# Two layers of a convolution network on one core: layer 1 moves into the bank of the input products, and steps move between ScalarE, VectorE and GpSimd

## The chip, the core and the metric

The kernel runs on one core of a Trainium2 chip. The metric is the device time of one execution in microseconds; the median of several executions counts. The core has a matrix engine (TensorE, PE in the rows), a vector engine (VectorE, DVE), a scalar engine (ScalarE, ACT) and GpSimd (POOL), each with its own queue that is worked off in order; SyncE (SP) starts transfers. The engines wait for each other by semaphores. Matrix products land in PSUM, eight banks of 512 float32 per partition.

## What is computed

The input x has 16 images of 128 channels and 128 x 128 pixels, float32. Cut to what matters:

```python
def _gn(v): ...            # mean and variance over groups of 4 channels and all pixels of an image

def layer0(x):             # x = _gn(x)
    xh = conv1x1(x, w_in, b_in)                       # 128 -> 256 channels
    pooled = jnp.mean(xh, axis=(2, 3))
    hcx = relu(pooled @ kg_w1.T + kg_b1)
    kernels = (hcx @ kg_w2.T + kg_b2)                 # a 3x3 kernel per image and channel
    y = depthwise_conv3x3(xh, kernels)
    y = y * jnp.tanh(softplus(y))                     # mish
    return conv1x1(y, w_out, b_out)                   # 256 -> 128

def layer1(x):             # x = _gn(x); FFT over channels, two 1x1 maps, inverse FFT
    return relu(real(ifft(...)))                      # linear up to the relu: one 128x128 matrix

x = x + layer0(_gn(x))
x = x + layer1(_gn(x))
```

## The kernel before

An image is a batch of 16 strips of 8 rows (1024 pixels); a half is 4 rows, 512 pixels. There are 256 strips n in all, and for each strip every engine runs one slot: `slot(n)` is written out for each engine by hand, and the order in it is the order of its queue. s = n % 16 is the strip's place in its batch. Layer 1 follows 19 strips behind: m = n - 19. Strips stay in SBUF (`X`, 23 places) from load to store.

The 256 hidden channels are split. The upper 128 get their nine taps as elementwise work on `xh`: the first three on ScalarE (`tap_product`, L407, into `tsum` and `tprod`), the two sums of these on GpSimd (`tap_add`, L1118), the other six on VectorE (`tap`, L907, in the two-bank `accB`). Of the lower 128 channels, the left SIDE = 56 of 128 columns are made the same way: ScalarE's `first_tap_side` (L416) and eight `side_tap` on VectorE (L919) in `accS`. The other 72 columns go through TensorE: `conv` (L654) multiplies the input, split in two float16 parts `hi` and `lo`, by tap matrices `wa` that hold kernel times input weight, three matmuls a tap, 27 a half.

The slot of TensorE for strip n, with the time-setting waits: `conv(n, 0)`; `layer1(m, 0)` (L705) into `psL`, waits for the ReLU before it; `product_out(n-1, 0)` (L696), the first layer's output product, into `psO`, waits for the Mishes of strip n-1 and the residual that read `psO` last; `product_b(n+2, 0)` (L674 to L676), the product of x, into `psB`; `conv(n, 1)` with `product_b(n+2, 1)` in its middle; `product_side(n+2)` (L685 to L687), also in `psB`; `layer1(m, 1)`; `product_out(n-1, 1)`. `psB` and `psO` are one bank each, and so is `psL`.

ScalarE's slot: `mish_side(n-1)` (L436), `first_tap_side(n)`, `mish_conv(n-1, 1)` (L429), `squares_1(n-2)` (L462), `tap_product(n+1, 0)` and `(n+1, 1)`, `mish_conv(n, 0)`, `relu(m, 0)` (L471), `sum_x` (L450), `evacuate(n+2, 0)` (L380, with an edge row L365 in some strips), `tap_product(n+1, 2)`, `squares_x` (L454), `evacuate(n+2, 1)`, `mish_taps(n)` (L442), `evacuate_side(n+2)` (L390), `relu(m, 1)`. VectorE's slot: `tap(n, 1)`, `residual(n-2, 1)` (L929), then side taps and taps in turn, `residual(n-1, 0)` between the sixth and the seventh side tap. GpSimd's slot: `add(m-1, 1)` (L1122), `cast(n+2)` (L1110), `tap_add(n+1, 1)`, `add(m, 0)`, `tap_add(n+1, 2)`, and the load of `hi` for strip n+3 (L1100).

In slots 10 to 15 of a batch, and slot 0 of the next, the weights for the next batch are made from its statistics: moments and group sums (10), the root on GpSimd (11), mean product and hidden layer (12: `pooled_products`, `hidden`), kernel products (13: `kernels`, L608), and three times `spread` (TensorE, L621), `tap_matrices` (VectorE, L876) and `taps_halves` (GpSimd: a float16 copy L1078 and the remainder L1080). In slots 1 to 3 the same goes on for layer 1's statistics. At the start, with nothing to overlap it, this chain is run once for batch 0, after `bn_stats` on 32 halves (L941). The last 16 strips of layer 1 are done behind the last slot.

## Time and profile before

| | us |
|---|---|
| median of 3 runs | 3799.29 |
| lowest, highest | 3797.97, 3801.11 |
| the profiled execution | 3798.16 |
| its span, first to last instruction | 3796.4 |

| engine | busy us | share of the span | instructions |
|---|---|---|---|
| TensorE | 3658.1 | 96% | 21868 |
| VectorE | 3522.8 | 93% | 4778 |
| ScalarE | 3316.2 | 87% | 5860 |
| GpSimd | 2774.9 | 73% | 2388 |

The busy time of an engine is the time in which at least one of its instructions was under way. Successive instructions overlap a little, so a row's duration is longer than what the instruction adds to its queue; the distance between two starts tells what it adds. Matmuls overlap most: their rows hold the way through the array. A row of a timeline ends in brackets with the idle time before it and who ended it, where there was some. Slots can be told apart by the second `product_out`, TensorE's last instruction of a slot.

### The profile page before, as it was taken

To read this page: it belongs to the slowest core of one execution; us is meant where nothing else is said; L and a number is where in the kernel's file an instruction comes from. 1 tells how busy PE (TensorE), PEld (TensorE's weight loads), DVE (VectorE), ACT (ScalarE), POOL (GpSimd) and SP (SyncE) were. 2 spreads that over 40 slices of the span, in tenths; PEclk is the share of its full clock that TensorE was granted. 3 is DMA by queue.
4 is the path that set the end of the run, shared out by engine and by line. 5 is a ranking of instruction groups with operands and counts; after the bars stand their busy time and mean duration, and the time that the engine had idled before them with its cause. 6 is when DMAs were issued, how large, how long until landed. Compare 5 with 4: busy or idle time off the path is not lost. (4 is left out here: it accounts for less than half of the span.)

```text
span 3796.4 us, 65618 instructions
## 1 busy us (share of the span) xinstructions
PE 3658.1 (96%) x21868; PEld 2251.8 (59%) x21868; DVE 3522.8 (93%) x4778; ACT 3316.2 (87%) x5860; POOL 2774.9 (73%) x2388
## 2 busy tenths in 40 slices
PE   4899999999999999999999999999999999999997
PEld 2455666656566666666656666565666656666664
DVE  5999999999999999999999999999999999999996
ACT  3888989899898998989999898998989989897775
POOL 3566777877778777777777777777777777777773
PEclk8999999999999999999999999999999999999999
DMA  4323444444444444444444444444444444443333
GB/s 152 78 70 104 130 128 132 125 130 131 122 139 119 137 127 127 136 122 132 126 128 132 128 130 125 131 133 123 134 128 129 130 125 134 125 131 95 92 94 126
DMA packets 148159, 468.99 MB, mean 124 GB/s; under 512 B 17328, under 2 KB 18416, under 8 KB 147568
## 3 DMA queue, kind: packets, MB, share of 16 engines
q1 hardware_dynamic: 110960, 397.66, 30.1%
q0 software_dynamic: 36864, 67.13, 12.2%
q8 instruction: 178, 2.92, 0.3%
q14 instruction: 157, 1.29, 0.1%
HBM read 397.61 MB, written 134.22 MB: 140 GB/s over the span
## 5 line engine op out<-in xcount | busy, mean ns | idle before, releaser
L654 PE MATMUL psA<-hi,wa 128*128 128x288 f16 (+4 forms) x9792 | 1852.2, 280 | 0.8 <-DVE wtmp L876 0.8
L907 DVE SCALAR_TENSOR_TENSOR accB<-xh,vectors,accB 128x1024 f32<-128x1024 f32 x1280 | 1640.4, 1282 | 0.0
L1118 POOL TENSOR_TENSOR tsum<-tsum,tprod 128x1024 f32<-128x1024 f32 x512 | 1210.5, 2364 | 293.9 <-ACT tprod L407 271.2
L919 DVE SCALAR_TENSOR_TENSOR accS<-side,vectors,accS 128x448 f32<-128x448 f32 x2048 | 1399.1, 683 | 19.2 <-ACT accS L416 10.0
L654 PE MATMUL psA<-lo,wa 128*128 128x288 f16 (+5 forms) x4896 | 1320.6, 279 | 0.0
L654 PEld LDWEIGHTS psA<-hi,wa 128*128 128x128 f16 x9792 | 931.0, 98 | 336.6 <-issue 66.9
L696 PE MATMUL psBO<-wm,woutt 128*128 128x512 f32 x2048 | 966.4, 594 | 12.5 <-DVE X L929 11.8
L1122 POOL TENSOR_TENSOR X<-X,zt 128x512 f32<-128x512 f32 x480 | 610.9, 1273 | 363.3 <-DVE accB L907 289.5
L696 PEld LDWEIGHTS psBO<-wm,woutt 128*128 128x128 f32 x2048 | 385.4, 190 | 497.5 <-issue 496.6
L1110 POOL TENSOR_TENSOR lo<-X,hi 128x1024 f16<-128x1024 f32 x256 | 546.9, 2136 | 182.6 <-DMA hi<-in_x_dram 111.4
L407 ACT ACTIVATE tprod<-xh,vectors 128x1024 f32<-128x1024 f32 x512 | 583.2, 1139 | 32.6 <-POOL tsum L1118 32.5
L654 PEld LDWEIGHTS psA<-lo,wa 128*128 128x128 f16 x4896 | 468.7, 98 | 238.2 <-issue 90.6
L705 PE MATMUL psL<-X,lpt 128*128 128x512 f32 x960 | 490.5, 592 | 2.3 <-ACT zt L471 2.3
L929 DVE SCALAR_TENSOR_TENSOR X<-psBO,vectors,X 128x512 f32<-128x512 f32 x512 | 382.5, 747 | 111.7 <-PE psBO L696 109.7
L380 ACT ACTIVATE xh<-psBO,vectors 128x512 f32<-128x512 f32 x510 | 348.7, 684 | 106.3 <-PE psBO L676 104.5
L907 DVE SCALAR_TENSOR_TENSOR accB<-xh,vectors,tsum 128x1024 f32<-128x1024 f32 x256 | 332.9, 1300 | 57.8 <-ACT wm L442 48.7
L471 ACT ACTIVATE zt<-psL,vectors 128x512 f32<-128x512 f32 x480 | 329.0, 685 | 42.1 <-PE psL L705 30.8
L407 ACT ACTIVATE tsum<-xh,vectors 128x1024 f32<-128x1024 f32 x256 | 290.7, 1136 | 3.9 <-DVE accB L907 3.4
L442 ACT ACTIVATE wm<-accB 128x1024 f32<-128x1024 f32 x256 | 261.8, 1023 | 27.9 <-DVE accB L907 27.0
L462 ACT ACTIVATE tprod<-X 128x1024 f32<-128x1024 f32 x256 | 270.5, 1057 | 13.3
L450 ACT ACTIVATE XS<-XS 128x1024 f32<-128x1024 f32 x240 | 252.8, 1053 | 3.8 <-DMA XS<-in_x_dram 3.7
L429 ACT ACTIVATE wm<-psA,vectors 128x284 f32<-128x284 f32 x480 | 231.1, 481 | 27.3 <-PE psA L654 26.6
(166 smaller groups left out, 3363.4 us busy)
## 6 DMA issues: line engine op xcount, KB each, us to landing
X<-in_x_dram SPq DMA_DIRECT2D x256, 512.0 KB, 3.3
out_dram<-X SPq DMA_DIRECT2D x256, 512.0 KB, 2.6
XS<-in_x_dram SPq DMA_DIRECT2D x240, 512.0 KB, 3.3
hi<-in_x_dram POOLq DMA_DIRECT2D x256, 256.0 KB, 4.3
X<-in_w_t_dram SPq DMA_DIRECT2D x2, 1152.0 KB, 18.3
w1t<-in_w_t_dram SPq DMA_DIRECT2D x1, 256.0 KB, 2.7
wint<-in_w_in_t_dram SPq DMA_DIRECT2D x1, 128.0 KB, 2.3
woutt<-in_w_out_t_dram SPq DMA_DIRECT2D x1, 128.0 KB, 2.6
```

The lines of the kernel that those rows point to most:

```text
L380: act(xh[:, r0:r0 + 4, 1:1 + W], ps, ACT.Identity, bias=b1).then_inc(s_xe, 1)
L407: act(rows_of(dst[:]), xh[:, 8 * j:8 * j + 8, k:k + W], ACT.Copy, scale=kk[i % 2][:, TAPS + k:TAPS + k + 1]).then_inc(done, 1)
L471: act(zt[:, t, :], psL[:], ACT.Relu, bias=lb[:, i % 2:i % 2 + 1]).then_inc(s_re, 1)
L654: last = mm(o[:, r:r + q, 0:cols], w, src[:, at:at + q, SIDE + dx - 1:SIDE + dx - 1 + cols], start=(tap == ORDER[0] and w is wh and src is ...
L696: last = mm(psO, woutt[:, h, :], wm[:, n % 2, h, t * TP:(t + 1) * TP], start=(h == 0), stop=(h == 1))
L705: mm(psL[:], lpt[:, i % 2, :], half(m, t), start=True, stop=True).then_inc(s_lm, 1)
L907: V.scalar_tensor_tensor(out=rows_of(accB[:]), in0=xh[:, 8 * j + dy:8 * j + dy + 8, dx:dx + W], scalar=kk[i % 2][:, TAPS + k:TAPS + k + 1] ...
L919: V.scalar_tensor_tensor(out=side_out(), in0=side[:, 8 * j + dy:8 * j + dy + 8, dx:dx + SIDE], scalar=kk[i % 2][:, k:k + 1], in1=side_out( ...
L929: V.scalar_tensor_tensor(out=half(n, t), in0=psO, scalar=boutp[:, 0:1], in1=half(n, t), op0=ALU.add, op1=ALU.add, accum_out=sum1[:, k:k + ...
L1110: P.tensor_tensor(lo[:, 8 * j:8 * j + 8, :], rows_of(strip(n)), hi[:, 8 * j:8 * j + 8, :], ALU.subtract).then_inc(s_lo, 1)
L1118: P.tensor_tensor(tsum[:], tsum[:], tprod[:], ALU.add).then_inc(s_ta, 1)
L1122: P.tensor_tensor(half(m, t), half(m, t), zt[:, t, :], ALU.add).then_inc(s_add, 1)
```

## The change

- SIDE goes from 56 to 60: 68 columns remain for TensorE, whose convolution matmuls have 272 columns instead of 288; side taps have 480 elements instead of 448, side products 488 columns instead of 456.
- `psO` becomes a tensor of two banks, and `residual` one operation on 1024 elements for two on 512. It runs in the place of the former half 1; `product_out` waits for it in half 0 alone.
- `psB` and `psL` become one bank, `psBL`. `product_b(n+2, 0)` waits for `relu(m, 0)`, and `layer1(m, 1)` for `evacuate_side(n+2)`. `product_out(n-1, 1)` goes ahead of `layer1(m, 1)`.
- The float16 copies of the tap matrices and input weights (`taps_halves`, `weights_halves`) move from GpSimd to ScalarE as `taps_high` and `weights_high`; GpSimd keeps the remainders, `taps_low` and `weights_low`.
- `tap_product(n+1, 1)` keeps its place before `mish_conv(n, 0)`, with `taps_high` before or behind it; `kernels_out` goes behind `mish_conv(n, 0)`; `small_0` behind the whole of `conv(n, 0)`.
- At the start the two loads of `w2t` go ahead of strips 2 to 15, and its copy and remainder ahead of the statistics' end. ScalarE's three `taps_high(0, u)` stand ahead of the first evacuations.
- Four `tensor_scalar` on GpSimd become `tensor_tensor` with a broadcast operand.

The diff, cut to its core:

```diff
-SIDE = 56
+SIDE = 60
@@
-        psBO = pb("psBO", [C, 2, TP])
-        psB, psO = psBO[:, 0, :], psBO[:, 1, :]
+        psO = pb("psO", [C, SP])
         accS = pb("accS", [C, TP])
-        psL = pb("psL", [C, TP])
+        psBL = pb("psBL", [C, TP])
+        psB, psL = psBL[:], psBL[:]
@@ sync
                 if n == 1:
                     for dst, src in consts:
                         eng.dma_start(dst, src).then_inc(s_const, 16)
-            for k in range(2):
-                eng.dma_start(w2t[:, k], w2_t[:, k]).then_inc(s_w2in[k], 16)
+                    for k in range(2):
+                        eng.dma_start(w2t[:, k], w2_t[:, k]).then_inc(s_w2in[k], 16)
@@ scalar
+            def taps_high(i, u):
+                eng.wait_ge(s_wt, 3 * i + u + 1)
+                act(wa[:, i % 2, 0, 3 * u * C:3 * (u + 1) * C], wtmp[:], ACT.Copy).then_inc(s_wsh, 1)
@@
-            stats_group("x", 0, small_bank(0))
-            pooled_out(0, small_bank(0))
-            hidden_out(0, small_bank(0))
             for k in range(2):
                 eng.wait_ge(s_w2in[k], 16)
                 act(w2p[:, 0, k], w2t[:, k], ACT.Copy).then_inc(s_w2h, 1)
+            stats_group("x", 0, small_bank(0))
+            pooled_out(0, small_bank(0))
+            weights_high(0)
+            hidden_out(0, small_bank(0))
             kernels_out(0, small_bank(0))
             bias_out(0, small_bank(0))
+            for u in range(3):
+                taps_high(0, u)
@@
                 if n + 1 < N:
                     tap_product(n + 1, 0)
+                if s == 0 and b >= 1:
+                    taps_high(b, 2)
+                if n + 1 < N:
+                    tap_product(n + 1, 1)
                 if s == 12 and build:
+                    weights_high(b + 1)
                     pooled_out(b + 1, small_bank(1))
                 if s == 3 and b >= 1:
                     layer1_bias(b - 1, small_bank(1))
-                if n + 1 < N:
-                    tap_product(n + 1, 1)
+                if s in (14, 15) and build:
+                    taps_high(b + 1, s - 14)
+                mish_conv(n, 0)
                 if s == 13 and build:
                     kernels_out(b + 1, small_bank(1))
-                mish_conv(n, 0)
@@ tensor, product_b
-                if bank is None:
+                if bank is None and t == 0 and n - 2 >= LAG1:
+                    eng.wait_ge(s_re, 2 * (n - 2 - LAG1) + 1)
+                elif bank is None:
                     eng.wait_ge(s_xe, 3 * n + t)
@@ product_out
-                if n + t >= 1:
-                    eng.wait_ge(s_x1, 2 * n + t)
+                if n >= 1 and t == 0:
+                    eng.wait_ge(s_x1, n)
@@ layer1
-                if m + t >= 1:
+                if t == 1 and m + LAG1 + 2 < N:
+                    eng.wait_ge(s_xe, 3 * (m + LAG1 + 2) + 3)
+                elif m + t >= 1:
                     eng.wait_ge(s_re, 2 * m + t)
@@ slot
-                conv(n, 0, slice(0, 5))
+                first = n % STRIPS == 0
+                conv(n, 0, slice(0, 6 if first else TAPS))
                 small_0(n)
-                first = n % STRIPS == 0
-                conv(n, 0, slice(5, 6 if first else TAPS))
@@
                     product_side(n + 2)
+                if n >= 1:
+                    product_out(n - 1, 1)
                 if m >= 0:
                     layer1(m, 1)
-                if n >= 1:
-                    product_out(n - 1, 1)
@@ vector
+                if c in (16, 20):
+                    k = (c - 16) // 4
+                    eng.wait_ge(s_w2h, k + 1)
+                    V.tensor_tensor(w2p[:, 1, k], w2t[:, k], w2p[:, 0, k], ALU.subtract).then_inc(s_w2l, 1)
@@
-            def residual(n, t):
-                eng.wait_ge(s_om, 2 * n + t + 1)
+            def residual(n):
+                eng.wait_ge(s_om, 2 * n + 2)
@@
-                    residual(n - 2, 1)
+                    residual(n - 2)
@@
-                if n >= 1:
-                    residual(n - 1, 0)
@@ gpsimd
-            def taps_halves(i, u):
-                k, part = 3 * i + u + 1, slice(3 * u * C, 3 * (u + 1) * C)
-                eng.wait_ge(s_wt, k)
-                P.tensor_copy(wa[:, i % 2, 0, part], wtmp[:]).then_inc(s_wsh, 1)
-                eng.wait_ge(s_wsh, k)
+            def taps_low(i, u):
+                part = slice(3 * u * C, 3 * (u + 1) * C)
+                eng.wait_ge(s_wsh, 3 * i + u + 1)
                 P.tensor_tensor(wa[:, i % 2, 1, part], wtmp[:], wa[:, i % 2, 0, part], ALU.subtract).then_inc(s_wsl, 1)
@@
                 eng.wait_ge(s_tap, NB * n + 1)
                 if s == 0 and b >= 1:
-                    taps_halves(b, 2)
+                    taps_low(b, 2)
```

TensorE's queue at the end of a slot, before. L685 to L687 are the side product, L705 is layer 1, L696 the output product, s_re counts ReLUs, s_xe evacuations and s_x1 residuals:

```order
L685 MATMUL psBO<-hi,wb 128x456 [waits s_xe]
L686 MATMUL psBO<-lo,wb 128x456
L687 MATMUL psBO<-hi,wb 128x456
L705 MATMUL psL<-X,lpt 128x512 [waits s_re]
L696 MATMUL psBO<-wm,woutt 128x512 [waits s_wS,s_x1,s_wB,s_wa]
L696 MATMUL psBO<-wm,woutt 128x512
L654 MATMUL psA<-hi,wa 128x288 [waits s_lo,s_wa]
```

The same place after the change:

```order
L704 MATMUL psBL<-hi,wb 128x488 [waits s_xe]
L705 MATMUL psBL<-lo,wb 128x488
L706 MATMUL psBL<-hi,wb 128x488
L715 MATMUL psO<-wm,woutt 128x512 [waits s_wS,s_wB,s_wa]
L715 MATMUL psO<-wm,woutt 128x512
L726 MATMUL psBL<-X,lpt 128x512 [waits s_xe]
L670 MATMUL psA<-hi,wa 128x272 [waits s_lo,s_wa]
```

Layer 1's second half has moved behind the output product and waits for the side's evacuation. In the middle of the slot, where half 0 of layer 1, half 0 of the output product and the first product of x follow each other, before:

```order
L705 MATMUL psL<-X,lpt 128x512 [waits s_re]
L696 MATMUL psBO<-wm,woutt 128x512 [waits s_wS,s_x1,s_wB,s_wa]
L696 MATMUL psBO<-wm,woutt 128x512
L674 MATMUL psBO<-hi,wb 128x512 [waits s_xe,s_lo]
L675 MATMUL psBO<-lo,wb 128x512
```

and after:

```order
L726 MATMUL psBL<-X,lpt 128x512 [waits s_re]
L715 MATMUL psO<-wm,woutt 128x512 [waits s_wS,s_x1,s_wB,s_wa]
L715 MATMUL psO<-wm,woutt 128x512
L693 MATMUL psBL<-hi,wb 128x512 [waits s_re,s_lo]
L694 MATMUL psBL<-lo,wb 128x512
```

The rows stand in the same order; the product of x waits for a ReLU in place of an evacuation. ScalarE's queue in slot 0 of a batch after the change; L415 are tap products, L354 is `taps_high`, L435 the convolution's Mish, L479 the ReLU of half 0:

```order
L444 ACTIVATE wm<-accS 128x8x60 [waits s_st,s_om]
L424 ACTIVATE accS<-side,vectors 128x480 [waits s_wS,s_kk,s_xe]
L435 ACTIVATE wm<-psA,vectors 128x4x68 [waits s_cv,s_om]
L470 ACTIVATE tprod,vectors<-X 128x1024 [waits s_ta,s_x1]
L415 ACTIVATE tsum<-xh,vectors 128x1024 [waits s_tap,s_kk,s_xe]
L354 ACTIVATE wa<-wtmp 128x384 [waits s_wt]
L415 ACTIVATE tprod<-xh,vectors 128x1024 [waits s_b1,s_kk,s_xe]
L435 ACTIVATE wm<-psA,vectors 128x4x68 [waits s_cv,s_om]
L479 ACTIVATE zt<-psBL,vectors 128x512 [waits s_add,s_lm]
```

The row of L354 is new there; before, the copy was GpSimd's first work of that slot.

## Rows read from the trace of the kernel before

**Rows 1.** The page, part 1: busy us, share of the span, instructions

```profile
PE 3658.1 (96%) x21868; PEld 2251.8 (59%) x21868; DVE 3522.8 (93%) x4778; ACT 3316.2 (87%) x5860; POOL 2774.9 (73%) x2388
```

**Rows 2.** Chain of waits, from 3600 to 3632: start us, us, what

```profile
3601.11 1.72 PE psBO L696 x4
...
3614.83 1.72 PE psBO L696 x4
```

**Rows 3.** Timeline of TensorE, last product of slots 19 and 253

```profile
359.07 1.88 PE L696 MATMUL psBO<-wm,woutt 128*128 128x512 f32 x4
...
3710.84 1.88 PE L696 MATMUL psBO<-wm,woutt 128*128 128x512 f32 x4
```

**Rows 4.** Timeline of ScalarE: start us, us, engine, line, operation [idle before]

```profile
1003.11 0.69 ACT L380 ACTIVATE xh<-psBO,vectors 128x512 f32<-128x512 f32 x1
...
1994.78 0.69 ACT L471 ACTIVATE zt<-psL,vectors 128x512 f32<-128x512 f32 x1
...
1998.34 1.14 ACT L407 ACTIVATE tsum<-xh,vectors 128x1024 f32<-128x1024 f32 x1
1999.38 1.13 ACT L407 ACTIVATE tprod<-xh,vectors 128x1024 f32<-128x1024 f32 x1
...
2000.95 0.68 ACT L471 ACTIVATE zt<-psL,vectors 128x512 f32<-128x512 f32 x1
...
2003.06 0.37 ACT L365 ACTIVATE xh<-psBO,vectors 128x128 f32<-128x128 f32 x1 [0.40 <-PE psBO L676]
...
2005.98 0.68 ACT L380 ACTIVATE xh<-psBO,vectors 128x512 f32<-128x512 f32 x1
```

**Rows 5.** Timeline of TensorE in the same stretches

```profile
1003.86 0.37 PE L685 MATMUL psBO<-hi,wb 128*128 128x456 f16 x1 [0.34 <-ACT xh L380]
...
1993.72 0.59 PE L705 MATMUL psL<-X,lpt 128*128 128x512 f32 x1
...
2002.21 0.38 PE L674 MATMUL psBO<-hi,wb 128*128 128x512 f16 x1
...
2007.44 1.02 PE L705 MATMUL psL<-X,lpt 128*128 128x512 f32 x2
```

**Rows 6.** Groups by line: form xcount | busy us, mean ns | idle before

```profile
L907 DVE SCALAR_TENSOR_TENSOR accB<-xh,vectors,accB 128x1024 f32<-128x1024 f32 x1280 | 1640.4, 1282 | 0.0
L919 DVE SCALAR_TENSOR_TENSOR accS<-side,vectors,accS 128x448 f32<-128x448 f32 x2048 | 1399.1, 683 | 19.2 <-ACT accS L416 10.0
...
L929 DVE SCALAR_TENSOR_TENSOR X<-psBO,vectors,X 128x512 f32<-128x512 f32 x512 | 382.5, 747 | 111.7 <-PE psBO L696 109.7
...
L621 PE MATMUL psA<-ident,vectors 128*128 128x128 f32 x288 | 42.2, 285 | 1.8 <-DVE wtmp L876 1.4 <-ACT vb L345 0.4
...
L608 PE MATMUL psA<-hv,w2p 128*128 128x2 f16 x576 | 30.6, 163 | 2.6 <-DVE w2p L949 2.6
```

**Rows 7.** Timeline of GpSimd in slot 0 of batch 4

```profile
992.87 0.50 POOL L1078 CAST wa<-wtmp 128x384 f16<-128x384 f32 x1 [2.85 <-DVE accB L907]
...
995.56 2.14 POOL L1110 TENSOR_TENSOR lo<-X,hi 128x1024 f16<-128x1024 f32 x1
997.66 2.36 POOL L1118 TENSOR_TENSOR tsum<-tsum,tprod 128x1024 f32<-128x1024 f32 x1
```

**Rows 8.** Busy us in windows (last three: clock, DMA share, GB/s); timelines, start

```profile
30.00:35.00 5.00, 0.00 (x0) 0.00 (x0) 5.00 (x9) 0.00 (x0) 0.00 (x0) 1.00 1.04 418
561.70:578.10 16.40, 15.35 (x89) 9.43 (x87) 16.23 (x25) 15.68 (x28) 13.17 (x22) 1.00 0.41 116
...
26.63 10.23 DVE L941 BATCH_NORM_STATS2 wm<-X 128x6 f32<-128x512 f32 x16 [0.32 <-DMA X<-in_x_dram]
...
50.70 5.03 DVE L949 TENSOR_TENSOR w2p<-X,w2p 128x2304 f16<-128x2304 f32 x2 [10.13 <-ACT w2p L490]
...
75.52 1.29 DVE L907 SCALAR_TENSOR_TENSOR accB<-xh,vectors,tsum 128x1024 f32<-128x1024 f32 x1 [7.63 <-POOL tsum L1118]
...
61.22 0.31 ACT L360 ACTIVATE xh<-vectors 128x130 f32<-128x130 f32 x1
```

More of the change, by code:

```diff
@@ L107, in conv_preact_kernel @@
         sumx, sqx = few(STRIPS), few(STRIPS)
-        sum1, sq1 = few(4 * STRIPS), few(STRIPS)
+        sum1, sq1 = few(2 * STRIPS), few(STRIPS)
         pooled = few(2)
@@ L242, in early_bank @@
         def early_bank(n, t):
-            return ((psB, psO), (psL[:], psA[:, 1, :]))[n][t]
+            return ((psB, psO[:, 0:TP]), (psO[:, TP:SP], psA[:, 1, :]))[n][t]
         def early_side(n):
@@ L249, in final_pair @@
         def final_pair(s):
-            return (accB[:], psA[:].rearrange("p t c -> p (t c)"), psBO[:].rearrange("p t c -> p (t c)"))[s % 3]
+            return (accB[:], psA[:].rearrange("p t c -> p (t c)"), psO[:])[s % 3]
         def final_z(s):
@@ L350, in bias_out, with weights_high @@
                 eng.wait_ge(s_beta, i + 1)
+            def taps_high(i, u):
+                eng.wait_ge(s_wt, 3 * i + u + 1)
+                act(wa[:, i % 2, 0, 3 * u * C:3 * (u + 1) * C], wtmp[:], ACT.Copy).then_inc(s_wsh, 1)
+            def weights_high(i):
+                eng.wait_ge(s_wn, i + 1)
+                act(wb[:, i % 2, 0, :], wn[:], ACT.Copy).then_inc(s_wbh, 1)
             def layer1_bias(i, ps):
@@ L457, in squares_1 @@
                 s = n % STRIPS
-                eng.wait_ge(s_x1, 2 * n + 2)
+                eng.wait_ge(s_x1, n + 1)
                 eng.wait_ge(s_ta, EXTRA * min(n + 3, N))
@@ L470, in relu @@
                     eng.wait_ge(s_add, 2 * m + t - 1)
-                act(zt[:, t, :], psL[:], ACT.Relu, bias=lb[:, i % 2:i % 2 + 1]).then_inc(s_re, 1)
+                act(zt[:, t, :], psL, ACT.Relu, bias=lb[:, i % 2:i % 2 + 1]).then_inc(s_re, 1)
             nc.scalar.preload_act_table_set("mish")
@@ L692, in product_out @@
                 eng.wait_ge(s_wS, n + 1)
-                if n + t >= 1:
-                    eng.wait_ge(s_x1, 2 * n + t)
+                if n >= 1 and t == 0:
+                    eng.wait_ge(s_x1, n)
                 for h in range(2):
-                    last = mm(psO, woutt[:, h, :], wm[:, n % 2, h, t * TP:(t + 1) * TP], start=(h == 0), stop=(h == 1))
+                    last = mm(psO[:, t * TP:(t + 1) * TP], woutt[:, h, :], wm[:, n % 2, h, t * TP:(t + 1) * TP], start=(h == 0), stop=(h == 1))
                 last.then_inc(s_om, 1)
@@ L702, in layer1 @@
                     eng.wait_ge(s_lpt, i + 1)
-                if m + t >= 1:
+                if t == 1 and m + LAG1 + 2 < N:
+                    eng.wait_ge(s_xe, 3 * (m + LAG1 + 2) + 3)
+                elif m + t >= 1:
                     eng.wait_ge(s_re, 2 * m + t)
-                mm(psL[:], lpt[:, i % 2, :], half(m, t), start=True, stop=True).then_inc(s_lm, 1)
+                mm(psL, lpt[:, i % 2, :], half(m, t), start=True, stop=True).then_inc(s_lm, 1)
             eng.wait_ge(s_const, 16 * len(consts))
@@ L846, in _ @@
             eng.wait_ge(s_wB, N)
-            eng.wait_ge(s_x1, 2 * N)
+            eng.wait_ge(s_x1, N)
             eng.wait_ge(s_lpt, B)
@@ L921, in side_tap @@
                                        op0=ALU.mult, op1=ALU.add).then_inc(s_st, 1)
-            def residual(n, t):
-                eng.wait_ge(s_om, 2 * n + t + 1)
-                i, s = n // STRIPS, n % STRIPS
-                if i >= 2 and s + t == 0:
+            def residual(n):
+                eng.wait_ge(s_om, 2 * n + 2)
+                i, k = n // STRIPS, n % (2 * STRIPS)
+                if i >= 2 and n % STRIPS == 0:
                     eng.wait_ge(hk["1mom"], i - 1)
-                k = i % 2 * 2 * STRIPS + 2 * s + t
-                V.scalar_tensor_tensor(out=half(n, t), in0=psO, scalar=boutp[:, 0:1], in1=half(n, t),
+                V.scalar_tensor_tensor(out=strip(n), in0=psO[:], scalar=boutp[:, 0:1], in1=strip(n),
                                        op0=ALU.add, op1=ALU.add, accum_out=sum1[:, k:k + 1]).then_inc(s_x1, 1)
@@ L946, in _ @@
             V.tensor_scalar(valid[:], valid[:], -1.0, None, ALU.add).then_inc(s_valid, 1)
-            for k in range(2):
-                eng.wait_ge(s_w2h, k + 1)
-                V.tensor_tensor(w2p[:, 1, k], w2t[:, k], w2p[:, 0, k], ALU.subtract).then_inc(s_w2l, 1)
             for u in range(3):
@@ L989, in _ @@
                 slot(n)
-            residual(N - 2, 1)
-            for t in range(2):
-                residual(N - 1, t)
+            residual(N - 2)
+            residual(N - 1)
             root_bits("1", B - 1)
@@ L1088, in fold_1 @@
             def fold_1(i):
[L1089 removed]
+                P.tensor_tensor(lpt[:, i % 2, :], lt[:], st["1"]["r"].broadcast_to([C, C]), ALU.mult).then_inc(s_lpt, 1)
             def high(n):
@@ L1134, in _ @@
             pool_bias(0)
-            weights_halves(0)
+            weights_low(0)
             hidden_low(0)
@@ L1138, in _ @@
             for u in range(3):
-                taps_halves(0, u)
+                taps_low(0, u)
             for k in range(1, EXTRA + 1):
@@ L1163, in slot @@
                 if s in (14, 15) and build:
-                    taps_halves(b + 1, s - 14)
+                    taps_low(b + 1, s - 14)
                 if m >= 0:
@@ L1177, in slot @@
                 if s == 12 and build:
-                    weights_halves(b + 1)
+                    weights_low(b + 1)
                 if s == 1 and b >= 1:
```

11 lines of the change are left out of this document (4 added, 7 removed).

## The prediction, made before the changed kernel was run

> **What bounds the kernel now.** I read the page first: TensorE is busy 96% of the span, VectorE 93%, ScalarE 87% [rows 1]. Then the chain of waits in a stretch late in the run: it is TensorE work from end to end, and the same product returns every 13.72 us (3601.11 to 3614.83) [rows 2]. So a normal slot lasts 13.73 us and TensorE sets it. The first layer's output product, of which a slot has two, I call out: 1.72 [rows 2].
>
> Next the ends of the slots, from the second out of each. Slot 19 ends at 360.95, slot 253 at 3712.72 [rows 3]: 234 slots in 3351.8 us. At 13.73 they would be 3212.8; the other 139 us lie in the slots that build the next batch's weights. That is about 10 us a batch.
>
> Last, what the engines do in one slot, since the change moves a wait. ScalarE runs without a gap from the ReLU of half 1 (1994.78) to the ReLU of half 0 of the next slot (2000.95): 6.17 us, and this is the smallest value found in any slot [rows 4]. TensorE goes from the first product of x (2002.21) over the second half of the convolution and the side product to layer 1 (2007.44) in 5.23 [rows 5]. Layer 1 starting at 1993.72 is followed by its ReLU at 1994.78: 1.06 us [rows 4, 5].
>
> **Narrower convolution, wider side.** 54 matmuls a slot go from 288 to 272 columns. The 5.23 us above hold six products of 512 columns, 27 convolution matmuls (18 of 288, 9 of 284) and three side products of 456: 12,180 columns, 5.08 us at 2.4 GHz (the clock is 1.00 [rows 8]). Nearly all of the time is columns, so of the bounds, 0 and 6.9 ns for 16 columns, I take 6.7: 0.18 us per 27 matmuls and 0.36 a slot, less 0.04 for three side products of 488 instead of 456. TensorE's own work would be 13.73 - 0.32 = 13.41. VectorE's eight side taps go from 448 to 480 elements: 448 take 683 ns and 512 take 747 in the nearest rows [rows 6], though of different inputs, so 32 more are 0.03 each, 0.26 a slot.
>
> **One residual of 1024 for two of 512.** An operation starts about 0.09 us before the one ahead of it ends (as 1998.34 + 1.14 against 1999.38 on ScalarE [rows 4]), so each counts its duration less 0.09: a tap 1.19, a side tap 0.59, a residual of 512 0.67 with the reading of its sum [rows 6]. One residual of 1024 elements has the length of a tap: the bounds are 1.19 and 2 x 0.67 = 1.34; I take 1.20, as a tap reads and writes as many elements. VectorE gains 0.14. Its own slot is 6 x 1.19 + 8 x 0.594 + 2 x 0.67 = 13.23 and becomes 13.35, with its small gaps about 13.5. That would bound the steady slots if nothing else did.
>
> **The shared bank.** This decides. Before, layer 1 had a bank of its own, and its ReLU could be late without holding any product of x. Now one bank is used in this order: layer 1 half 0 of strip m, its ReLU, product of x half 0, its evacuation, half 1, its evacuation, side product, its evacuation, layer 1 half 1, its ReLU. And layer 1 half 1 now stands behind the second out. Follow one turn, from a ReLU of half 1 to the next one:
> 1. ScalarE reaches the next ReLU of half 0 after 6.17 [rows 4]. In between are the side's Mish and first tap, now 480 wide (0.03 more each), and two convolution Mishes, 0.015 less each: 6.20.
> 2. That ReLU lasts 0.685 (0.68 and 0.69) [rows 4].
> 3. TensorE's product of x now waits for it. Where TensorE waits for ScalarE, the matmul begins 0.055 after the end in the closest cases: an evacuation ends at 1003.80, the side product starts at 1003.86 [rows 4, 5].
> 4. From product of x to the end of the side product 5.23, less 0.18, plus 0.04: 5.09.
> 5. The second out, now ahead of layer 1: 1.72 [rows 2].
> 6. Layer 1 to its ReLU: 1.06.
> The sum is 14.81 us. All queues are in order, so nothing on them can pass. Behind TensorE's wait of step 3 stand the second half of the convolution, the other products of x and out; behind ScalarE's wait for layer 1 stand the side's Mish and first tap, and behind those VectorE's side taps. Every slot pays the turn: 1.08 more than 13.73. A second turn runs through ScalarE up to the evacuation of half 1: from the ReLU of half 0 to it 5.03 (2000.95 to 2005.98) [rows 4], of which 0.40 was waiting, 0.1 the overlap that a wait takes away, and 0.27 an edge row: 4.26 without. It ends 0.685 later; then 0.055, 0.63 for the side product, 1.72 and 1.06: 6.20 + 4.26 + 0.685 + 3.465 = 14.61, and 14.88 in one slot of four with an edge row there. Averaged, the slot is 14.82.
>
> TensorE then idles 1.4 us a slot ahead of the product of x and VectorE 1.3; the gains of the first two edits are hidden under that wait. 234 slots at 14.82 are 3467.9.
>
> **The steps that build weights.** In these slots all that lies on the turn adds. ScalarE's conversion of three taps (384 elements) is not in the trace; between 0.31 (130 elements, 61.22) [rows 8] and 0.64 (448 elements) I take 0.58, near the latter, of which 0.47 from start to start. TensorE's kernel products are 1.9 a batch (30.6 over 16), a spread 0.9 (42.2 over 48) [rows 6], 0.67 of it beyond what it overlaps; the hidden layer's few small products I put at the same 0.9. By slot of the batch: 10: moments and group product 0.7. 12: upper halves 0.36, copy 0.17, hidden 0.9: 1.4. 13: kernel products end 0.46 after the ReLU would, bias rows 0.6: 1.1. 14: 0.47 + 0.67 and the wait for VectorE's second table: 1.2. 15: 1.0, the border tile being smaller. 1: 0.7. 3: 0.5, as GpSimd starts late after its fourteen short steps. Slot 0 is the dear one. GpSimd began its last three taps at 992.87, when VectorE's tap was done [rows 7]; now it must wait for ScalarE's conversion, behind the first tap product. That starts 3.56 after the ReLU of half 1 (1998.34) [rows 4], 3.46 with the border's single Mish; 1.04 and 0.58 more make 5.1. From GpSimd's conversion to its cast 2.69, less 0.58 of conversion, is 2.1, the cast 2.1, the sum 2.36 [rows 7]: ScalarE's last tap product can start at 11.8 instead of 8.8, and the slot takes 18.0, 3.2 more. Together 9.8 a batch, 14 batches: 138. (Before: 10.3. What the new order saves in slots 3 and 12 to 15 it loses in slot 0.) I allow 5 to 14.
>
> **The start.** The two weight loads now go ahead of strips 2 to 15. 2 x 1152 KB at 418 GB/s [rows 8] take 5.6 us. VectorE ended its statistics at 36.86, having run since 26.63 without waiting; now strip 7 is in at 31.9, and two subtractions (5.03) and eight strips (10.23) follow: 47.1, 10.2 later. Given back is about 2.8: the kernel products began when the subtractions ended (50.70 + 5.03) [rows 8], and will now begin when the first products of x are done. ScalarE's evacuations began at 61.22; in the new order they stand behind the last conversion, 68.5, so the first tap (75.52) comes not 7.4 but 12.6 later: 5.9 of evacuations and products, then two sums of 2.36 and a product of 1.14 [rows 6, 8]. I take +12.6, bounds +7 and +16. Slots 0 to 19, mostly VectorE's: +2 (0 to 6). The tail's instructions are the same: 0.
>
> **The sum.** 3467.9 + 138 - 3351.8 = +254.1; +12.6; +2: +268.7. On the profiled execution, 3798.16 (span 3796.4), that is 4066.9; the median of the runs is 1.1 higher, 3799.29. I say 4067. The slot is good to 0.1 (23 us), the weight slots to -70 and +57, the start to 6.
>
> **A page against the trace: the clock.** In the window from 561.7 to 578.1 TensorE idles 1.05 us, waiting for a weight slot's small product, and the clock is 1.00 [rows 8]. The new gap is 1.4 in every slot. The Trainium skill, "TensorE: Matmul & The Clock Gate", Part 1, has the array drop to half its rate once it has idled. If 1.4 us did that, the clock would be 0.5 in steps 4 to 6 and their 7.7 us would double: 22.5 a slot, some 5860 us. The trace speaks against it; 2%.
>
> **Rivals.**
> - *Only VectorE's turn binds.* ReLU of half 1, side Mish, first side tap, five taps and five side taps, last Mish, side evacuation, layer 1: 0.58 + 0.68 + 0.76 + 9.2 (five taps of 1.19, five side taps of 0.63) + 0.09 + 0.92 + 0.72 + 1.06 = 14.0. If the product of x found its ReLU done, 234 x 0.3 = 70, plus 15: 3885. Against it: ScalarE has no time to give between the two ReLUs [rows 4]. 12%.
> - *Faster.* If the turn is shorter than 13.5 us, VectorE's own work binds. It needs 1.3 us off the turn, from the ReLU being released early or out not standing in it. 234 x (13.5 - 13.73) = -54, start +15, weight slots up to -40: 3720 to 3760. For it: TensorE's work does fall by 0.32. Against it: step 1 is the shortest of all slots and the rest are back-to-back rows. 6%.
> - *The weight slots cost double.* A late sum on GpSimd delays VectorE's first tap of the following slot as well: 20 a batch, 4205. 5%.
> - *Forecast*, 75%.
>
> **Chances.** A run of this kernel can tell about 0.2% from no change. Slower 0.93, within 0.2% 0.01, faster 0.06. The range: 4067 less 70 and 23 partly offset gives 3990; plus 57 and some of the double case 4135.
>
> **What would show it.** A normal slot of 14.8; TensorE idle 1.4 ahead of each product of x, put down to the ReLU; out directly after the side product; ScalarE idle about 2 us ahead of the ReLU of half 1; VectorE idle 1.3 ahead of its first side tap; slot 0 near 18; first tap near 88. Slots of 14.0 with TensorE waiting only at layer 1 mean the first rival, slots of 13.5 that I read the order of the bank wrongly, a clock of 0.5 the page.

## The result, and the profile after

| | before | after |
|---|---|---|
| median, us | 3799.43 | 4063.65 |
| lowest, highest | 3797.97, 3801.11 | 4058.71, 4069.47 |
| profiled execution, span | 3798.16, 3796.4 | 4064.72, 4062.9 |
| ends of slots 19, 253, 255 | 360.95, 3712.7, 3739.2 | 374.0, 3974.1, 3997.8 |

The ratio is 1.069, 95% interval 1.068 to 1.071: slower, as forecast, and 3 us below the forecast. The page of after, part 1 and the chain's shares, against [rows 1]:

```profile
PE 3642.1 (90%) x21868; PEld 2242.1 (55%) x21868; DVE 3589.0 (88%) x4266; ACT 3307.9 (81%) x5924; POOL 2753.2 (68%) x2324
...
PE 47%; ACT 25%; issue 14%; POOL 5%; DVE 1%; ACTq 1%; POOLq 0%; DVEq 0%
```

Each engine is busy about as long as before, and none is near the whole span. The chain, TensorE from end to end in [rows 2], now changes engines: that is what a turn of waits looks like. The waits of after (engine, line, what it waited for, us, times, longest):

```profile
...
ACT zt L479 <- PE psBL L726: 426.2, 241, 3.0
...
DVE accS L939 <- ACT accS L424: 281.2, 241, 2.0
PE psBL L693 <- ACT zt L479: 244.8, 206, 2.0
...
POOL wa L1095 <- ACT wa L354: 122.4, 18, 7.9
```

L479 is the ReLU, L726 layer 1, L424 the first side tap, L693 the first product of x, L354 `taps_high`, L1095 `taps_low`. A wait of TensorE for the ReLU ahead of the product of x did not exist before. (The row left out ahead of these is GpSimd's addition, which waits 559.8 for the ReLU.) ScalarE's timeline over one turn, from a ReLU of half 1 to the next (start, us, what, idle before):

```profile
3872.07 0.69 ACT L479 ACTIVATE zt<-psBL,vectors 128x512 f32<-128x512 f32 x1 [1.68 <-PE psBL L726]
...
3873.93 0.46 ACT L437 ACTIVATE wm<-psA,vectors 128x268 f32<-128x268 f32 x1
3874.30 0.26 ACT L438 ACTIVATE wm<-psA,vectors 128x4 f32<-128x4 f32 x1
3874.44 1.05 ACT L470 ACTIVATE tprod<-X 128x1024 f32<-128x1024 f32 x1
...
3878.08 0.69 ACT L479 ACTIVATE zt<-psBL,vectors 128x512 f32<-128x512 f32 x1
...
3886.80 0.69 ACT L479 ACTIVATE zt<-psBL,vectors 128x512 f32<-128x512 f32 x1 [1.91 <-PE psBL L726]
```

And TensorE's in it:

```profile
3878.91 0.38 PE L693 MATMUL psBL<-hi,wb 128*128 128x512 f16 x1 [1.14 <-ACT zt L479]
...
3883.81 0.37 PE L706 MATMUL psBL<-hi,wb 128*128 128x488 f16 x1
3884.02 1.88 PE L715 MATMUL psO<-wm,woutt 128*128 128x512 f32 x4
3885.74 0.59 PE L726 MATMUL psBL<-X,lpt 128*128 128x512 f32 x1
```

The six steps can be read off: ReLU of half 1 to ReLU of half 0 6.01; the ReLU 0.69; 0.14 to the product of x; 5.11 to the output product; 1.72; 1.06 to the next ReLU: 14.73.

VectorE at the start of batch 0, where the predicted delay showed: the subtractions (L961) now stand between the statistics, and the first tap is at 88.48 instead of 75.52 [rows 8]:

```profile
33.36 2.54 DVE L961 TENSOR_TENSOR w2p<-X,w2p 128x2304 f16<-128x2304 f32 x1
...
38.20 2.54 DVE L961 TENSOR_TENSOR w2p<-X,w2p 128x2304 f16<-128x2304 f32 x1
40.65 7.22 DVE L964 BATCH_NORM_STATS2 wm<-X 128x6 f32<-128x512 f32 x12
...
88.48 1.29 DVE L927 SCALAR_TENSOR_TENSOR accB<-xh,vectors,tsum 128x1024 f32<-128x1024 f32 x1 [12.64 <-POOL tsum L1131]
```

**Slot 0 holds something I had not expected.** TensorE's rows in slot 48 (slot 0 of batch 3) and slot 64 (slot 0 of batch 4), where the product of x waits for `lo` from GpSimd:

```profile
811.82 0.39 PE L693 MATMUL psBL<-hi,wb 128*128 128x512 f16 x1 [2.09 <-POOL lo L1123]
...
1057.43 0.61 PE L693 MATMUL psBL<-hi,wb 128*128 128x512 f16 x1 [2.09 <-POOL lo L1123]
1057.83 0.63 PE L694 MATMUL psBL<-lo,wb 128*128 128x512 f16 x1
```

The wait is the same, but in slot 64 the product of x takes 0.61 instead of 0.39. Windows (us, busy of PE, PEld, DVE, ACT, POOL, then granted clock, DMA share, GB/s) of most of slot 48 and of parts of slot 64:

```profile
800.00:818.00 18.00, 14.13 (x77) 8.04 (x76) 15.12 (x20) 13.40 (x22) 10.29 (x7) 1.00 0.32 89
...
1054.00:1055.00 1.00, 0.89 (x8) 0.75 (x9) 1.00 (x2) 0.04 (x1) 1.00 (x2) 1.00 0.00 0
...
1056.00:1057.00 1.00, 0.00 (x0) 0.00 (x0) 1.00 (x2) 1.00 (x2) 1.00 (x1) 0.50 0.87 356
...
1061.00:1062.00 1.00, 1.00 (x6) 0.69 (x5) 0.46 (x1) 0.99 (x2) 0.92 (x1) 0.50 0.00 0
```

In slot 64 the granted clock falls to 0.50, which is 1.2 GHz, during that wait, and is back at 1.00 before 1063. Of the 14 slots 0 between slots 20 and 253 two ran at 1.00 (2.4 GHz) throughout and took 17.86; in twelve the clock fell, and they took 18.44 to 20.05, together 14.6 us more than twelve times 17.86.

### The profile page after: what moved, and what is told of

It reads as the page before. It is cut to its first block, busy times and chain, and to the rows that moved or that the text cites. A ratio compares the mean times of both kernels' runs of the same rounds, so it can differ in the third digit from the quotient of the medians.

```text
span 4062.9 us, 64851 instructions
## 1 busy us (share of the span) xinstructions
PE 3642.1 (90%) x21868; PEld 2242.1 (55%) x21868; DVE 3589.0 (88%) x4266; ACT 3307.9 (81%) x5924; POOL 2753.2 (68%) x2324
## 3 DMA queue, kind: packets, MB, share of 16 engines
q14 instruction: 153, 1.25, 0.1%
## 4 chain that ended last, share of the span: by engine, by line
PE 47%; ACT 25%; issue 14%; POOL 5%; DVE 1%; ACTq 1%; POOLq 0%; DVEq 0%
PE psA L670 18%; PE psO L715 10%; ACT tprod L415 6%; PE psBL L726 5%; ACT tprod L470 5%; ACT wm L437 4%; PE psBL L693 3%; ACT zt L479 3%; ACT wm L444 3%; PE psBL L694 2%; PE psBL L695 2%; POOL tsum L1131 2%; ACT wm L438 1%; PE psBL L704 1%; POOL lo L1123 1%
## 5 line engine op out<-in xcount | busy, mean ns | idle before, releaser
L670 PE MATMUL psA<-hi,wa 128*128 128x272 f16 (+4 forms) x9792 | 1766.8, 275 | 19.5 <-POOL wa L1095 18.8
L939 DVE SCALAR_TENSOR_TENSOR accS<-side,vectors,accS 128x480 f32<-128x480 f32 x2048 | 1474.3, 720 | 299.2 <-ACT accS L424 281.2
L670 PE MATMUL psA<-lo,wa 128*128 128x272 f16 (+5 forms) x4896 | 1298.4, 275 | 0.0
L1135 POOL TENSOR_TENSOR X<-X,zt 128x512 f32<-128x512 f32 x480 | 609.6, 1270 | 562.5 <-ACT zt L479 559.8
L715 PE MATMUL psO<-wm,woutt 128*128 128x512 f32 x2048 | 964.3, 593 | 2.3 <-DVE X L948 1.2
L479 ACT ACTIVATE zt<-psBL,vectors 128x512 f32<-128x512 f32 x480 | 330.8, 689 | 426.2 <-PE psBL L726 426.2
L415 ACT ACTIVATE tprod<-xh,vectors 128x1024 f32<-128x1024 f32 x512 | 584.3, 1141 | 33.5 <-POOL tsum L1131 33.1
L715 PEld LDWEIGHTS psO<-wm,woutt 128*128 128x128 f32 x2048 | 388.4, 190 | 398.0 <-issue 359.2
L726 PE MATMUL psBL<-X,lpt 128*128 128x512 f32 x960 | 496.4, 599 | 6.7 <-ACT zt L479 5.2
L693 PE MATMUL psBL<-hi,wb 128*128 128x512 f16 x509 | 196.3, 386 | 301.2 <-ACT zt L479 244.8
L388 ACT ACTIVATE xh<-psBL,vectors 128x512 f32<-128x512 f32 x509 | 347.9, 683 | 68.5 <-PE psBL L695 66.7
L948 DVE SCALAR_TENSOR_TENSOR X<-psO,vectors,X 128x1024 f32<-128x1024 f32 x256 | 327.8, 1280 | 29.8 <-PE psO L715 28.4
L693 PEld LDWEIGHTS psBL<-hi,wb 128*128 128x128 f16 x509 | 53.4, 105 | 493.0 <-issue 370.1
L415 ACT ACTIVATE tsum<-xh,vectors 128x1024 f32<-128x1024 f32 x256 | 292.0, 1141 | 3.8 <-DVE accB L927 3.4
```

Source lines behind the costliest of these rows:

```text
L415: act(rows_of(dst[:]), xh[:, 8 * j:8 * j + 8, k:k + W], ACT.Copy, scale=kk[i % 2][:, TAPS + k:TAPS + k + 1]).then_inc(done, 1)
L479: act(zt[:, t, :], psL, ACT.Relu, bias=lb[:, i % 2:i % 2 + 1]).then_inc(s_re, 1)
L670: last = mm(o[:, r:r + q, 0:cols], w, src[:, at:at + q, SIDE + dx - 1:SIDE + dx - 1 + cols], start=(tap == ORDER[0] and w is wh and src is ...
L693: mm(o, wb[:, i % 2, 0, C:HID], xhi, start=True, stop=False)
L715: last = mm(psO[:, t * TP:(t + 1) * TP], woutt[:, h, :], wm[:, n % 2, h, t * TP:(t + 1) * TP], start=(h == 0), stop=(h == 1))
L726: mm(psL, lpt[:, i % 2, :], half(m, t), start=True, stop=True).then_inc(s_lm, 1)
```

## The experiments

All ratios are against the kernel before, on the same chip. Slots are distances between the ends of second output products, as in [rows 3].

### The bank alone, and everything but the bank

The first kernel is before with the whole bank part: `psO` of two banks, one `residual` of 1024, `psBL` with its waits, and layer 1's second half behind the second output product. SIDE stays 56:

```diff
-        psBO = pb("psBO", [C, 2, TP])
-        psL = pb("psL", [C, TP])
+        psO = pb("psO", [C, SP])
+        psBL = pb("psBL", [C, TP])
@@ product_b
+                if bank is None and t == 0 and n - 2 >= LAG1:
+                    eng.wait_ge(s_re, 2 * (n - 2 - LAG1) + 1)
@@ slot: product_out(n - 1, 1) ahead of layer1(m, 1)
```

> The kernel before with the bank part alone: one bank for products of x and layer 1, two banks and one residual of 1024, layer 1 half 1 behind the second output product. 56 side columns, halves on GpSimd, old start. Theory of the turn: the 27 wider matmuls in it cost 0.14 more than in the changed kernel and the side 0.03 less, so a normal slot is 14.83, longer than the 14.72 of the changed kernel though VectorE has less to do; slot 0 of a batch about 1.5 over a normal one instead of 3.1; start as before; total about 4010. Rival, VectorE sets the pace: slot below 14.5.

Measured: 4042.2, ratio 1.063 (1.061 to 1.065). The slot is 14.82, as expected: the steps are 5.98, 0.69, 0.14, 5.23, 1.72 and 1.06. The total is 32 above the expected 4010. From slot 19 to slot 253 the trace has 3590.5, which is 234 times 14.82 and 122.6 more; the expected total leaves some 90 for this (3802 and 234 times 1.10 are 4059, 49 above 4010, and before has 139). Slots 0 are only 0.45 over a normal one, but slots 13 take 16.9 to 18.6. The tail is 6.2 longer. Its TensorE waits for the ReLU at the same place:

```profile
3902.09 0.38 PE L677 MATMUL psBL<-hi,wb 128*128 128x512 f16 x1 [0.94 <-ACT zt L471]
```

The second is the changed kernel with these lines undone (the same diff backwards, on after).

> The changed kernel without its bank part: psB, psO and psL are one bank each again, two residuals of 512, layer 1 ahead of the output product, waits as before. Kept: 60 side columns, ScalarE's upper halves, the new start. Theory of the turn: no ReLU holds a product of x, so a normal slot falls to VectorE's own work, 13.2 + 0.26 and small gaps, 13.5 to 13.65; slot 0 of a batch stays about 3 dearer and the start 13 later; total 3775 to 3805. Rival, the wider side or ScalarE's new work makes the slots slow: total above 4000.

Measured: 3815.9, ratio 1.0035 (1.0023 to 1.0048); normal slots of 13.43 to 13.63, mostly 13.63, as expected. The total lies 11 above the range. Two things in the trace make up most of that: slot 19 ends at 377.4 (16.5 later than before, not 13), and slot 0 takes 16.8, or 17.5 to 17.7 where the clock falls, in eight cases of 14. So the bank part costs 240 us without the other edits (4042 - 3802) and 248 with them (4064 - 3816). It holds the shared bank, the order behind it and the single residual together. The next experiments vary the order; a shared bank with two residuals of 512 was not run.

### The order in the shared bank

```diff
+                if m >= 0:
+                    layer1(m, 1)
                 if n >= 1:
                     product_out(n - 1, 1)
-                if m >= 0:
-                    layer1(m, 1)
```

> The changed kernel with one thing undone: layer 1 half 1 stands ahead of the second output product again, in the shared bank. Theory of the turn (ScalarE's ReLU of half 1, 6.2 us to the ReLU of half 0, product of x to side product 5.1, output product 1.7, layer 1 to its ReLU 1.06): the output product leaves the turn, the side's evacuation (about 0.9 with its two hand-overs) comes into it, slot 14.72 to about 14.1, where VectorE's own turn (14.0) binds too; total about 3920 us. Rival, that VectorE's wider side and the single residual set the pace (88% busy): slot stays 14.7, total 4060.

Measured: 4129.6, ratio 1.086 (1.084 to 1.088); slots of 15.0, and 15.2 with an edge row, where 14.1 was expected. A clear miss: taking the 1.72 of the output product out of the turn made the slot longer. VectorE's timeline shows where it waits:

```profile
3919.86 1.28 DVE L948 SCALAR_TENSOR_TENSOR X<-psO,vectors,X 128x1024 f32<-128x1024 f32 x1 [1.48 <-PE psO L715]
...
3935.06 1.28 DVE L948 SCALAR_TENSOR_TENSOR X<-psO,vectors,X 128x1024 f32<-128x1024 f32 x1 [1.48 <-PE psO L715]
```

The residual needs the second half of the output product. Where that product is late, VectorE stands still ahead of the residual, with five more taps and all side taps behind it; the Mish of the taps waits for them, the side's evacuation for ScalarE, layer 1 for the evacuation (TensorE waits 1.27 there), the output product for layer 1, and the next residual for that. This turn (wait 1.48, VectorE's own work 13.7) was in none of my cases. In the kernel before a residual stands at the same place and waits for the same product:

```profile
1996.49 0.75 DVE L929 SCALAR_TENSOR_TENSOR X<-psBO,vectors,X 128x512 f32<-128x512 f32 x1 [0.27 <-PE psBO L696]
```

But there layer 1, ahead of that product in the queue, waits for no evacuation of the side, so the turn is not closed and the wait is 0.27. What closes it, as the queues stand, is that wait in the shared bank. The residual of 1024 is longer than one of 512 (1.28 against 0.75), and it stands on the turn; how much of the 15.2 it adds, no run shows.

The other direction, both output products ahead of the product of x:

```diff
                     product_out(n - 1, 0)
+                    product_out(n - 1, 1)
@@
-                if n >= 1:
-                    product_out(n - 1, 1)
```

> The changed kernel with the second output product moved once more: both stand together in the middle of the slot, ahead of the product of x, where TensorE idles 1.4 us for the ReLU. The shared bank and all its waits stay. Theory of the turn: the 1.72 us of the output product fill that idle time and leave the turn; layer 1 half 1 then waits for the side's evacuation (0.93), and the longest way is TensorE's own round 0.86 + 3.17 + 0.86 + 3.44 + 5.09 + 0.93 = 14.35, 0.2 more where an edge row is copied: slot 14.35 to 14.5 against 14.72, total about 3980 us. VectorE's residual gets its product early, so it does not bind as it did with layer 1 first. Rival, that sharing the bank costs the same wherever the output product stands: slot 14.7, total 4060.

Measured: 4032.1, ratio 1.0605 (1.058 to 1.063); normal slots 14.43 to 14.68 against an expected 14.35 to 14.5, the total 52 above the expected 3980. The longer normal slots are part of that; more lies in single slots: slot 0 falls to 14.57, but slot 1 rises to 18.16 and slot 13 to 17.12. In a normal slot TensorE now waits once, ahead of layer 1 (us in total, times, longest):

```profile
PE psBL L726 <- ACT side L398: 208.0, 235, 1.5
```

Its own work (13.43 in the kernel with separate banks) and this wait, 0.96 in the slot looked at, make 14.4: the two output products fill what had been the wait for the ReLU, and the evacuation of the side ahead of layer 1 is then the price of the bank.

### Whose work lies on the turn

One statement of ScalarE's between the two ReLUs shortened: the squares for layer 1's statistics on one column instead of 1024. Only this part of layer 1's statistics is left out.

```diff
-                act(tprod[:], strip(n), ACT.Square,
+                act(tprod[:, 0:1], strip(n)[:, 0:1], ACT.Square,
```

> The changed kernel with ScalarE's squares of layer 1's input (L470) made on one column instead of 1024: that part of the statistics is left out. It takes 0.8 us out of ScalarE's way from the ReLU of half 1 to the ReLU of half 0. Theory of the turn: slot 14.72 less 0.8 is 13.9, and VectorE's turn of 14.0 binds instead: 14.0 to 14.1, total about 3900. Rival, ScalarE is not in the way (81% busy): slot stays 14.7, total 4060.

Measured: 3918.3 (one execution); normal slots 13.85 to 14.26, 0.45 to 0.85 less than with the squares, where 13.9 to 14.1 and a total of 3900 were expected. ScalarE's work between the ReLUs is on the turn.

One of VectorE's side taps shortened, in the changed kernel; seven of its eight rows are left out:

```diff
-                V.scalar_tensor_tensor(out=side_out(), in0=side[:, 8 * j + dy:8 * j + dy + 8, dx:dx + SIDE],
+                r = 1 if k == 2 else 8
+                V.scalar_tensor_tensor(out=side_out()[:, 0:r], in0=side[:, 8 * j + dy:8 * j + dy + r, dx:dx + SIDE],
```

> The changed kernel with one of the eight side taps (the third, k = 2) on one row of 60 elements instead of eight rows of 480; the other seven rows of that tap are left out. VectorE's work falls by some 0.45 us a slot, ScalarE's and TensorE's stay. Theory (the turn runs through ScalarE between its two ReLUs, and from the first ReLU through TensorE: product of x, side product, output product, layer 1): VectorE is not on it, so the normal slot stays at 14.70 to 14.76 and only weight slots can shorten; 4040 to 4064. Rival (VectorE's row of taps between two waits sets the pace): 0.45 off every slot, 14.25 to 14.3, some 3960.

Measured: 4061.1 (one execution), slots 14.70 to 14.76, unchanged, though VectorE is busy 108 us less. The page's first line, against that of after above:

```profile
PE 3636.5 (90%) x21868; PEld 2242.5 (55%) x21868; DVE 3480.9 (86%) x4266; ACT 3310.3 (82%) x5924; POOL 2751.9 (68%) x2324
```

VectorE is not on the turn, and the first rival of the prediction falls. The same cut in the kernel with layer 1 first, where its trace puts VectorE on the turn:

> The kernel with layer 1's second half ahead of the second output product, and the same short side tap (seven of its eight rows left out). That kernel took 4129.6 with slots of 15.0 and 15.2. Theory, read from its trace: there the turn runs through VectorE: the residual waits for the output product, which stands behind layer 1, and the first side tap for the residual; so 0.45 comes off every slot, 14.55 to 14.75, some 4020 to 4035. Rival (it is ScalarE or GpSimd that sets its pace, and VectorE's wait at the residual is only a consequence): 15.0 to 15.2 stays, over 4110.

Measured: 4954.1. In this execution the granted clock is 0.75 almost throughout from 96.8 us on, which nothing in the kernel explains, and normal slots are 18.4 to 18.6. So it was run again:

> The same kernel once more (layer 1's second half ahead of the second output product, and one side tap on one of its eight rows, the other seven left out). In its first execution TensorE's granted clock stood at 0.75 from 96.6 us to the end, where the same program with whole side taps had 1.00, and it took 4954.1. If that clock belonged to that execution, the clock is 1.00 now and the time is what the theory of the turn through VectorE gives: slots of 14.55 to 14.75, 4020 to 4035. If the kernel itself brings the clock down, it is 0.75 and some 4950 again, and nothing is learned on the turn.

Measured: 4097.3 (4 executions, 4094.1 to 4097.9), ratio 1.077 (1.075 to 1.079), and the clock is 1.00 in the normal slots. These are 14.69 and 14.94 instead of 15.0 and 15.2: 0.3 less, not 0.45. The total is 32 less than with the whole tap, where some 100 was expected: slots 0, 1 and 12 to 15 are no shorter, so that tap is not on their turn. For the normal slots the sign bears VectorE's turn out, and the size suggests that the next one lies close behind. Its ScalarE, late in the run:

```profile
3906.98 1.06 ACT L470 ACTIVATE tprod<-X 128x1024 f32<-128x1024 f32 x1 [0.56 <-DVE X L949]
```

The squares wait for the residual too, and the ReLU of half 0 stands behind them. Residual 3905.65, squares 3906.98, ReLU of half 0 3910.63, product of x 3911.45, side product from 3915.93 to 3916.72, its evacuation 3916.76, layer 1 3917.48, output product 3918.44, and the next residual is due at 3920.34: 14.69. That this second turn binds is read from one slot and was not tried by itself.

### The start, and the conversion on ScalarE

Before, with the new place of the loads, the copy and the subtraction of `w2t` alone:

```diff
+                    for k in range(2):
+                        eng.dma_start(w2t[:, k], w2_t[:, k]).then_inc(s_w2in[k], 16)
@@ vector
+                if c in (16, 20):
+                    k = (c - 16) // 4
+                    V.tensor_tensor(w2p[:, 1, k], w2t[:, k], w2p[:, 0, k], ALU.subtract).then_inc(s_w2l, 1)
```

> The kernel before with the new place of the two weight loads alone, and of their copy on ScalarE and subtraction on VectorE (ahead of strips 2 to 15, within the statistics). Theory: statistics end 10.2 later, 2.8 comes back, so the first tap starts 7.4 later and the total is 3802 + 7 = 3809; the other 5 us of the changed kernel's start come from the evacuations standing behind ScalarE's conversions. Rival, the loads account for the whole later start: total 3815 to 3818. Rival, no cost, because the loads only change places: 3802.

Measured: 3808.4, ratio 1.0018 (1.0008 to 1.0027). The first tap is at 83.77, 8.25 late (expected 7.4), and slot 19 ends at 369.3, 8.4 late. Of the 13 us that the changed kernel loses at the start, 8.3 come from here. The 4.7 left fit the three conversions: in after ScalarE's first evacuation starts at 76.31, behind the last of them (75.88), and here at 70.03. They were not taken out by themselves.

Last, the changed kernel with separate banks, the old start, and GpSimd's own float16 copies for batch 0 and for the third table of each batch; ScalarE keeps the copies in slots 12, 14 and 15:

```diff
-                if s == 0 and b >= 1:
-                    taps_high(b, 2)
@@ gpsimd, s == 0
-                    taps_low(b, 2)
+                    taps_halves(b, 2)
```

> The kernel with own banks for layer 1 and 60 side columns, the old start, and GpSimd's float16 copy for batch 0 and for the third table of each batch (slot 0); ScalarE keeps the copies in slots 12, 14 and 15. Theory: slot 0 falls from 17.6 to about 14.8 (14 times), the start by 16, normal slots stay 13.63: 3816 - 39 - 16 = about 3762 us, 1% under the kernel before. Rival, GpSimd's copy is not what made slot 0 dear: 3800.

Measured: 3765.9, ratio 0.9904 (0.9889 to 0.9919): about 1% faster than before, and clear of noise. Slot 0 takes 14.67 instead of 16.8 to 17.7, slot 19 ends at 363.5. A normal slot, from one second output product to the next:

```profile
3582.71 1.95 PE L707 MATMUL psBO<-wm,woutt 128*128 128x512 f32 x4
...
3596.34 1.95 PE L707 MATMUL psBO<-wm,woutt 128*128 128x512 f32 x4
```

13.63, which is VectorE's own work: in a normal slot with 60 side columns and separate banks its rows have no idle time. To balance the two engines the side was made narrower in it:

```diff
-SIDE = 60
+SIDE = 58
```

> The same with 58 side columns instead of 60. Theory: at 60 VectorE sets the normal slot (13.63) while TensorE needs 13.43; at 58 VectorE needs 13.50 and TensorE 13.57, so the slot is 13.55 to 13.6: 5 to 15 us less than with 60. Rival, the pace is set by something else than VectorE's side taps: no difference or TensorE's 0.14 more.

Measured: 3770.0, ratio 0.9916 (0.9899 to 0.9932), no gain where 5 to 15 us were expected. Normal slots are 13.56 to 13.59. With 60, some slots behind the weight slots run at TensorE's 13.43 and the others at 13.63, so that both kernels come to the same average of about 13.6. Why VectorE does not bind in the short ones was not looked into.

## Why the prediction was right

| part | predicted | measured |
|---|---|---|
| normal slot | 14.82 | 14.70 to 14.76 |
| weight slots, us a batch over normal | 9.8 | 9.85, without the clock |
| half clock in slots 0 | not in it | +14.6 |
| slots 20 to 253 | 3605.9 | 3600.1 |
| slot 19's end, over before | +14.6 | +13.05 |
| slots 254 and 255, and the tail | 0 | -2.8 and +7.9 |

**The bound and the turn.** The mechanism held in every step, and the bank kernel shows it without the other edits: 14.82 against 13.73. Two steps were mis-sized. Step 1 was put at 6.20 and is 6.01. I took the stretch in before for one without a gap, but there the squares start 0.32 after the row of the border's Mish, and in after 0.14 (3874.30 to 3874.44). The rows of before, ScalarE's and the residual's:

```profile
1996.97 0.26 ACT L430 ACTIVATE wm<-psA,vectors 128x4 f32<-128x4 f32 x1
1997.29 1.06 ACT L462 ACTIVATE tprod<-X 128x1024 f32<-128x1024 f32 x1
...
1997.17 0.08 DVE L929 DVE_READ_ACCUMULATOR X<-psBO,vectors,X 128x1 f32 x1
```

That is a pause of 0.17, without a bracket, while ScalarE waited for the residual of half 1, done at 1997.25. Step 3 was put at 0.055 and is 0.144 in all normal slots. The side product behind an evacuation, which still starts 0.055 after it, was the wrong model for the product of x behind a ReLU; why the two differ is open. Step 4 is 5.12 against 5.09, the others exact. Together -0.08 a slot, about -20 us.

**The narrower convolution** is worth 5.23 - 5.12 = 0.11 on the turn (predicted 0.14), and 14.82 - 14.73 = 0.09 of the slot. Where separate banks leave TensorE alone it is worth 0.3: 13.43.

**The second turn** through the evacuation of half 1, put at 14.88 in one slot of four, sets the pace in slots 2, 5, 6 and 9, which have an edge row in either half: 14.75 against 14.70 in slots 4 and 8. Slot 69, ScalarE and then TensorE:

```profile
1134.37 0.69 ACT L479 ACTIVATE zt<-psBL,vectors 128x512 f32<-128x512 f32 x1
...
1138.96 0.68 ACT L388 ACTIVATE xh<-psBL,vectors 128x512 f32<-128x512 f32 x1
...
1139.70 0.38 PE L704 MATMUL psBL<-hi,wb 128*128 128x488 f16 x1
```

That evacuation ends at 1139.64, and the side product starts 0.06 later; in the turn shown above, without an edge row, it starts 0.54 after the evacuation. From the ReLU of half 0 to the evacuation it is 4.59 where I had 4.53, and step 1 is 6.01 instead of 6.20; that brings 14.88 down to 14.75.

**The weight slots.** By slot, over the normal one: 10 0.65, 12 1.2, 13 1.25, 14 1.05, 15 1.1, 0 3.1, 1 0.8, 3 0.7, against 0.7, 1.4, 1.1, 1.2, 1.0, 3.2, 0.7 and 0.5. The times given for slot 0 add up to 11.7, not the 11.8 used. In slot 0 GpSimd waits 7.79 for ScalarE's conversion, and the product of x 2.09 for GpSimd's `lo`. What I missed is what that idle time does to the clock: I weighed the gap of every slot, 1.14 here, and found no fall; I did not ask the same of the longest gap, which my own working of slot 0 implied. It costs 14.6 us; only the width of the range for these slots covers it.

**The start**: statistics end at 47.9 (47.1), first tap 88.48 ("near 88"), +13.0 (+12.6). Slots 0 to 19 add nothing beyond it (+2).

**The end.** "The tail's instructions are the same" was true and not enough: the last two slots are 2.8 shorter, the tail 7.9 longer. In the bank kernel the tail is 6.2 longer, so most of that belongs to the bank. From 4000 to 4010 the clock is 0.66, and two products of layer 1 take 2.0 there where 1.0 to 1.1 is usual.

In sum: -20 for the turn, 0 for the weight slots, +15 for the clock, -2 for the start, +5 for the end, and the profiled execution lies at 4064.7 against 4066.9. So part of the closeness is luck, in that errors cancelled: the slot's and the clock's are each larger than what is left.

**The rivals.** Only VectorE's turn: fell by the shortened side tap. Faster: the turn was not shorter than 13.5; but the estimate for that case, 13.5 and 3720 to 3760, is close to what the kernel with separate banks and GpSimd's copies gives, 13.63 and 3766. Weight slots at double cost: no. Half clock in every slot: no; in twelve of 14 slots 0, yes.

## What to carry to other kernels

When two producers share a buffer, write down the whole turn (every holder of it, and what stands ahead of each on its in-order queue) and add it up from start-to-start distances: here no engine is busy more than 90% of the span after the change, and the slot still grew by 1.0. An idle stretch counts as zero only by the distance of starts against the same pair elsewhere, not by the absence of a bracket. And a new wait on one queue can close a turn through another engine, so the order that takes a step out of one turn can lengthen another: with layer 1 first, its wait for the evacuation made VectorE's residual late, and the slot longer.
